# Causal attention on one core: masks as the last products of their step, other tiles behind V

## The chip, the cores and the metric

The kernel runs on one core of a Trainium2 chip. The metric is the device time of one execution in microseconds. The core has five engines with queues of their own: TensorE (PE in the profile; PEld are its weight loads), VectorE (DVE), ScalarE (ACT), GpSimd (POOL) and SyncE (SP), which here only issues DMAs. Each takes its instructions in the order in which they were written and waits on semaphores for the others.

## What is computed

Two half-weight feed-forward layers around an attention layer, on 4 sequences of 1024 tokens with 128 features, all in fp32:

```python
x = x + 0.5 * ffn(layernorm(x), w_gate, w_up, w_down)     # silu(gate) * up, 384 hidden
x = x + attn(layernorm(x), wq, wk, wv, wo)
x = x + 0.5 * ffn(layernorm(x), w_gate, w_up, w_down)

# attn: 16 heads of 64, rotary embedding on q and k
scores = einsum('bhid,bhjd->bhij', q, k) * 64 ** -0.5
scores = where(tril(ones(T, T)), scores, -inf)
probs = softmax(scores)
out = einsum('bhij,bhjd->bhid', probs, v)
return einsum('bto,do->btd', out, wo)
```

## The kernel before

The feed-forward layers (`macaron_half`) are not touched. The change is in `attention`. It works on 32 pairs of heads, 8 for each sequence, in a loop over i with an inner u of 0 and 1 (pair p is 2i + u). Everything is stored transposed: keys in the partitions, queries in the columns.

A pair has 12 **steps** (`STEPS`), numbered from 0. A step takes one block of 128 keys and one half of the queries (512 columns, or fewer where the causal mask cuts them: `first_col`). Steps 0 to 3 belong to the first half, 4 to 11 to the second. In each step TensorE computes, for both heads (h is 0 and 1), the scores of the block into `scores[h]`, one PSUM bank for each head: a **high** product (L541; rounded keys times both parts of the queries) and a **low** product (L547; it also brings in the negated row maximum as a 65th row). In steps 0, 1, 2, 3, 6, 8, 10 and 11 (`DIAG`) the block crosses the diagonal, and a third product (L544), 16-bit, of 128 columns, adds -1e30 above it: the **mask**. Their order in a masked step is high, high, mask, mask, low, low. The low products release ScalarE (`scores_full`), which takes the exponentials of the two heads (L679), and these (`probs_done`) release the banks for the next step's high products. The widths of the score products in steps 0 to 11 are 512, 384, 128, 256, 512, 512, 128, 512, 256, 512, 384 and 512 columns.

Two steps later (`LAG`) the probabilities meet **V** (`times_v`, L567): products of 64 output columns of the array for each head, in fp32, side by side. GpSimd adds the probabilities up (L858 to L862), `sum_probs` (L577) sums them over the keys, `project_out` (L586) is the output projection of a half.

Between these lies work for the pairs ahead:
- **max tiles** (`max_unit`, L530) compute high scores of the next pair once more, with the queries in the partitions, and VectorE takes their row maxima (L752 for a full tile, L756 for one on the diagonal). They are numbered 0 to 25. Units 8 and 25 (`ROWS_UNIT`, L525) transpose the maxima into rows, which VectorE negates (L766) and SyncE sends into the 65th row (`send_max`, L933). The tiles use two banks in turn, so unit k waits until VectorE is through with unit k-2.
- **projections** of q and k for the pair after next (`project`, L504 to L506), rotated by VectorE (L733 to L745), rounded by ScalarE (`round_high`, L659, behind steps 6 and 8) and split by GpSimd (L840); in even pairs (u is 0) four projections of V (L514 to L516), kept by ScalarE (L668).

The tables `MAX_AHEAD`, `MAX_BEHIND`, `MAX_LATE`, `PROJ_AT` and `V_AT` say in which step which unit comes, and `pair` of each engine puts them in order: ahead is between the scores and V, behind is after V.

SyncE's queue for one pair is, in order: `fill_qk(.., 0)` (8 DMAs, L908 and L909, as soon as the scores of the pair before are done), `send_max(p, u, 1)`, which waits for unit 25's negation, `fill_qk(.., 1)` (8), `fill_low` (4, L914 and L915), `copy_v`, `load_wo`, loads, `send_max(p + 1, 1 - u, 0)`. `round_high` writes the tile from which the fills read, so in step 6 it waits for all of them. On ScalarE it is followed by `invert` (L686, L690) and the exponentials of step 7.

Of the kernel before, what the change touches and what calls it, by code (L numbers as in the profile page):

```python
# [21 lines left out]
P = 128  # L22
# [369 lines left out]
def attention(nc, x, xn_dram, xn_stored, wo_pairs, ahead_of, cos, sin, tables_arrived, constants,  # L392
              probs_mem, v_stage, banks):
    ones64, tri_mask, ident, ident16, mask16 = constants
# [3 lines left out]
    with ctx:  # L398
# [54 lines left out]
                     [(1, h, i + b, k) for h in range(2) for i in (4, 6) for k in range(2) for b in range(2)] + [(1, None, None, None)])  # L453
        NT = len(MAX_UNITS)
        ROWS_UNIT = [8, NT - 1]
        MAX_AHEAD = {4: (2, 3), 5: (6, 7), 6: (8, 9), 7: (11,), 8: (13,), 10: (18,), 11: (20, 21)}
        MAX_BEHIND = {3: (0, 1), 4: (4, 5), 6: (10,), 7: (12,), 8: (14, 15), 9: (16, 17), 10: (19,), 11: (22,)}
        MAX_LATE = (23, 24)
        N_QK, N_LOW, N_SENT = 16 * 8, 16 * 4, 16 * 2

        PROJ_AT = {0: 0, 1: 1, 2: 2, 3: 3, 5: 4, 6: 5}
        ROUND_AT, LOW_AT = {6: 0, 8: 1}, {7: 0, 9: 1}
        V_AT = {(0, 7): 0, (0, 8): 1, (0, 9): 2, (0, 11): 3}

        def probs_of(s):
            slot = s % SLOTS
# [2 lines left out]
        def first_col(s):  # L469
            c, j = STEPS[s]  # L470
            return max(0, P * (j - 4 * c))
# [20 lines left out]
        def _(pe):  # L492
# [40 lines left out]
            def score(p, i, u, s):  # L533
                c, j = STEPS[s]
                x0 = first_col(s)
                keys, q = slice(j * P, (j + 1) * P), slice(c * CHUNK + x0, (c + 1) * CHUNK)

                def with_high(h):
                    if some(2 * NS * p + 2 * s + h - 1):
                        pe.wait_ge(probs_done, 2 * NS * p + 2 * s + h - 1)  # L540
                    nc.tensor.matmul(scores[h][:, x0:], k_hh[u][h][:, keys], q_hl[u][h][:, q], start=True, stop=False)  # L541

                def with_mask(h):
                    nc.tensor.matmul(scores[h][:, x0:x0 + P], ident16[:], mask16[:], start=False, stop=False)  # L544

                def with_low(h):
                    nc.tensor.matmul(scores[h][:, x0:], k_l1[u][h][:, keys], q_hm[u][h][:, q], start=False,  # L547
                                     stop=True).then_inc(scores_full, 1)

                if s in DIAG:  # L550
                    for part in (with_high, with_mask, with_low):
                        for h in range(2):
                            part(h)
                else:
                    for h in range(2):
                        with_high(h)
                        with_low(h)

            def times_v(p, u, s):
                c, j = STEPS[s]  # L560
# [20 lines left out]
            def project_out(p, i, u, c):  # L581
                if c == 0:
                    pe.wait_ge(wo_loaded[u], 16 * (i + 1))
                pe.wait_ge(head_done, 2 * p + c + 1)
                pe.wait_ge(norm_free, 4 * p + 2 * c + 1)
                nc.tensor.matmul(norm_bank[:], wo_cur[:, u, :], head_out[:, c, :], start=True, stop=True).then_inc(norm_full, 1)  # L586

            def pair(i, u, first, last):
                p = 2 * i + u
                has_prev, has_next, has_next2 = not (first and u == 0), not (last and u == 1), not last  # L590
                for s in range(NS):
                    if s == 0:
                        if first:
                            pe.wait_ge(ones_done, 4)
                        pe.wait_ge(filled_low[u], N_LOW * (i + 1))
                        pe.wait_ge(v_copied[u], 16 * (i + 1))
                        pe.wait_ge(max_sent[u][0], N_SENT * (i + 1))
                    if s == 4:
                        pe.wait_ge(max_sent[u][1], N_SENT * (i + 1))
                    score(p, i, u, s)  # L600
                    if s == 0 and has_prev:
                        for k in MAX_LATE:
                            max_unit(p, i, u, k)
                    if s == 1 and has_prev:
                        max_unit(p, i, u, ROWS_UNIT[1])
                    if has_next:
                        for k in MAX_AHEAD.get(s, ()):
                            max_unit(p + 1, i + u, 1 - u, k)
                    if s == 4 and has_prev:
                        project_out(p - 1, i - 1 + u, 1 - u, 1)  # L610
                    if s == 8:
                        project_out(p, i, u, 0)
                    if s >= LAG:
                        times_v(p, u, s - LAG)
                    elif has_prev:
                        times_v(p - 1, 1 - u, s - LAG + NS)
                    if s == 2 and has_prev:
                        sum_probs(p - 1, 1)
                    if s == 6:
                        sum_probs(p, 0)  # L620
                    if has_next:
                        for k in MAX_BEHIND.get(s, ()):
                            max_unit(p + 1, i + u, 1 - u, k)
                    if s in PROJ_AT and has_next2:
                        project(i + 1, u, PROJ_AT[s])
                    if (u, s) in V_AT and has_next2:
                        project_v(i + 1, V_AT[u, s])

# [495 lines left out]
```

## Time and profile before

| | |
|---|---|
| median of 3 runs | 1355.13 us (1354.36 to 1357.69) |
| the profiled execution | 1354.49 us, of which the trace's span is 1352.8 us |
| TensorE busy | 1288.6 us, 95% |
| VectorE busy | 871.6 us, 64% |
| GpSimd busy | 752.1 us, 56% |
| ScalarE busy | 618.7 us, 46% |
| mean granted TensorE clock | 0.975 of full |

Times below are microseconds from the start of the span. A row of the instructions in order of time has its start, its length, the engine, the line, and what it writes and reads; rows of the same kind that follow each other are merged (x2), and their length is then from the first start to the last end. The length of a product includes its way through the array, so products overlap in the rows; how far apart they start is what they cost. Attention lies between about 150 and 1240 us. `ident` and `mask` of L544 are the 16-bit tiles.

### The profile page before, as it was taken

The page shows a single profiled execution, that of the slowest core. Times are in us where ns is not written, and L with a number is a line of the kernel's source. Part 1 is how long each engine was busy: PE and PEld are TensorE (multiplying, and loading weights), DVE is VectorE, ACT ScalarE, POOL GpSimd, SP SyncE. Part 2 cuts the span into 40 slices and gives each one's busy share as a digit, 9 for nine tenths or more (in the row PEclk, how much of TensorE's full clock was granted, in tenths as well). Part 3 has the DMA queues.
Part 4 walks back from the last instruction along what each step waited for, and adds up shares of the span by engine and source line. Part 5 has one row for each costly group of instructions (what it writes and reads, how often), then busy time and mean ns, then how long its engine had stood idle before and what let it go on. Part 6 is the DMA issues. An engine that isn't in the chain of part 4 may idle for free. (4 is left out here: it accounts for less than half of the span.)

```text
span 1352.8 us, 24949 instructions
## 1 busy us (share of the span) xinstructions
PE 1288.6 (95%) x6240; PEld 737.4 (55%) x6240; DVE 871.6 (64%) x2270; ACT 618.7 (46%) x1176; POOL 752.1 (56%) x454
## 2 busy tenths in 40 slices
PE   5986689999999999999999999999999999999798
PEld 2543455555555555555555655555555555555365
DVE  5565557767676767676767676767676767664254
ACT  3654134444444444444444444444444444444474
POOL 4123146666666656566666666666666666665300
PEclk8998599999999999999999999999999999999899
DMA  7022556555555646464646464646464646452001
GB/s 280 33 93 72 155 119 159 119 145 132 131 145 120 156 112 163 111 157 118 158 107 163 105 161 107 163 107 162 104 165 105 160 107 162 107 121 56 0 24 39
DMA packets 113612, 165.86 MB, mean 123 GB/s; under 512 B 13360, under 2 KB 63408, under 8 KB 113456
## 3 DMA queue, kind: packets, MB, share of 16 engines
q1 hardware_dynamic: 113584, 165.53, 48.0%
q8 instruction: 12, 0.20, 0.1%
q14 instruction: 16, 0.13, 0.0%
HBM read 37.29 MB, written 10.49 MB: 35 GB/s over the span
## 5 line engine op out<-in xcount | busy, mean ns | idle before, releaser
L862 POOL TENSOR_TENSOR psum_p<-psum_p,shared_a 128x256 f32<-128x256 f32 (+1 forms) x192 | 280.9, 1463 | 93.9 <-ACT shared_a L679 84.4
L679 ACT ACTIVATE shared_a<-bank 128x512 f32<-128x512 f32 (+3 forms) x512 | 201.5, 445 | 240.4 <-PE bank L547 232.8
L530 PE MATMUL bank<-k_hh,q_hl 128*128 128x512 f32 (+3 forms) x768 | 258.7, 392 | 9.7 <-DVE rotated L745 4.2
L547 PE MATMUL bank<-q_hm,k_l 65*128 65x512 f32 (+3 forms) x768 | 243.5, 371 | 0.0
L752 DVE TENSOR_REDUCE max_left<-bank 128x1 f32<-128x512 f32 x256 | 175.7, 687 | 93.3 <-PE bank L530 93.2
L530 PEld LDWEIGHTS bank<-k_hh,q_hl 128*128 128x128 f32 x768 | 138.1, 192 | 173.5 <-issue 72.9
L541 PE MATMUL bank<-q_hl,k_hh 128*128 128x512 f32 (+3 forms) x768 | 227.2, 349 | 0.7 <-ACT shared_a L679 0.5
L679 ACT ACTIVATE probs_more<-bank 128x512 f32<-128x512 f32 (+1 forms) x256 | 132.1, 568 | 191.1 <-PE bank L547 176.8
L756 DVE CUSTOM_DVE_ANT_0 max_scratch<-bank,tri_mask,max_left 128x128 f32<-128x128 f32 (+3 forms) x256 | 137.9, 548 | 109.6 <-PE bank L530 109.6
L567 PE MATMUL bank<-shared_a,v_cur 128*64 128x512 f32 (+3 forms) x1024 | 201.1, 471 | 0.0
L840 POOL TENSOR_TENSOR parts<-rotated,parts 128x1024 fp32r<-128x1024 f32 x64 | 152.4, 2381 | 58.0 <-ACT parts L659 58.0
L860 POOL TENSOR_TENSOR psum_p<-probs_more 128x1024 f32<-128x1024 f32 x32 | 76.1, 2380 | 142.6 <-ACT probs_more L679 142.6
L862 POOL TENSOR_TENSOR psum_p<-psum_p,probs_more 128x768 f32<-128x768 f32 x64 | 134.7, 2105 | 24.4 <-ACT probs_more L679 21.5
L541 PEld LDWEIGHTS bank<-q_hl,k_hh 128*128 128x128 f32 x768 | 131.6, 190 | 24.0 <-ACT shared_a L679 5.9
L756 DVE CUSTOM_DVE_ANT_0 max_scratch<-bank,tri_mask 128x128 f32<-128x128 f32 (+3 forms) x256 | 118.4, 488 | 40.8 <-PE bank L530 39.2
L567 PE MATMUL bank<-probs_more,v_cur 128*64 128x512 f32 (+1 forms) x512 | 131.0, 591 | 0.0
L547 PEld LDWEIGHTS bank<-q_hm,k_l 65*128 65x128 f32 x768 | 126.0, 191 | 7.4
L738 DVE TENSOR_TENSOR bank<-bank,cos 128x256 f32<-128x256 f32 x128 | 54.6, 427 | 77.3 <-PE bank L506 77.2
L567 PEld LDWEIGHTS bank<-shared_a,v_cur 128*64 128x64 f32 x1024 | 50.6, 134 | 92.7 <-ACT probs_more L679 33.1
L659 ACT ACTIVATE parts<-rotated 128x1024 fp32r<-128x1024 f32 x64 | 67.7, 1059 | 68.7 <-DMA q_hm<-parts 56.4
L860 POOL TENSOR_TENSOR psum_p<-shared_a 128x768 f32<-128x768 f32 x32 | 58.4, 1825 | 73.0 <-ACT shared_a L679 73.0
L504 PEld LDWEIGHTS bank<-xn_cur,w_qk 128*128 128x128 f32 x192 | 37.6, 196 | 84.9 <-issue 35.7
(126 smaller groups left out, 1923.0 us busy)
## 6 DMA issues: line engine op xcount, KB each, us to landing
q_hl<-parts SPq DMA_DIRECT2D x256, 128.0 KB, 2.8
k_hh<-parts SPq DMA_DIRECT2D x256, 128.0 KB, 2.7
xn_cur<-xn_scratch SPq DMA_DIRECT2D x16, 1024.0 KB, 6.4
k_l<-parts SPq DMA_DIRECT2D x64, 256.0 KB, 4.9
q_hm<-parts SPq DMA_DIRECT2D x64, 256.0 KB, 5.0
v_cur<-shared_b SPq DMA_DIRECT2D x32, 512.0 KB, 6.0
w_qk<-w_scratch SPq DMA_DIRECT2D x32, 256.0 KB, 3.1
w_scratch<-first_w_parts SPq DMA_DIRECT2D x8, 512.0 KB, 3.1
```

The lines of the kernel that those rows point to most:

```text
L530: nc.tensor.matmul(max_bank[k % 2][:, 0:w], q_hl[u][h][:, q * P:(q + 1) * P], k_hh[u][h][:, keys * CHUNK:keys * CHUNK + w], start=True, st ...
L541: nc.tensor.matmul(scores[h][:, x0:], k_hh[u][h][:, keys], q_hl[u][h][:, q], start=True, stop=False)
L547: nc.tensor.matmul(scores[h][:, x0:], k_l1[u][h][:, keys], q_hm[u][h][:, q], start=False, stop=True).then_inc(scores_full, 1)
L567: last = nc.tensor.matmul(out_bank[c][HEAD_DIM * h:HEAD_DIM * (h + 1), x0:], v_cur[:, u, j, HEAD_DIM * h:HEAD_DIM * (h + 1)], probs_of(s)[ ...
L659: nc.scalar.activation(parts[:, 0, :, c * CHUNK:(c + 1) * CHUNK], rotated[c][:], ACT.Copy).then_inc(high_done, 1)
L679: nc.scalar.activation(probs_of(s)[:, h, x0:], scores[h][:, x0:], ACT.Exp, scale=SCORE_SCALE).then_inc(probs_done, 1)
L738: nc.vector.tensor_tensor(bank[:, w:2 * w], bank[:, 0:w], cos[:, cols], ALU.mult).then_inc(by_cos_done, 1)
L752: nc.vector.reduce_max(max_left[:, col], max_bank[k % 2][:], AX.X).then_inc(max_free, 1)
L756: nc.vector.tensor_tensor_reduce(out=max_scratch[k % 2][:, 0:w], in0=max_bank[k % 2][:, 0:w], in1=tri_mask[:, CHUNK - w:], scale=1.0, scal ...
L840: nc.gpsimd.tensor_tensor(parts[:, 1, :, cols], rotated[c][:], parts[:, 0, :, cols].bitcast(F32), ALU.subtract).then_inc(low_done, 1)
L860: last = nc.gpsimd.tensor_tensor(acc, probs_of(s - 1)[:, :, x0:], new, ALU.add)
L862: last = nc.gpsimd.tensor_tensor(acc, acc, new, ALU.add)
```

## The change

In a masked step the low product of a head now directly follows its high product, as in unmasked steps, and the two masks come last, with the signal to ScalarE. Directly behind them comes V of two steps before. What stood between the scores and V moves: the max tiles of step 0 (23 and 24) and the transposed rows of step 1 (unit 25) go behind V, and so do units 8 and 9 in step 6, and 13 and the output projection in step 8. In steps 10 and 11 one max tile (17, 20) stays ahead, between the low products and the masks. To even this out tiles are dealt out anew in steps 4 to 11. The fourth projection of V moves from step 11 to step 10.

```diff
-        MAX_AHEAD = {4: (2, 3), 5: (6, 7), 6: (8, 9), 7: (11,), 8: (13,), 10: (18,), 11: (20, 21)}
-        MAX_BEHIND = {3: (0, 1), 4: (4, 5), 6: (10,), 7: (12,), 8: (14, 15), 9: (16, 17), 10: (19,), 11: (22,)}
+        MAX_AHEAD = {4: (2, 3), 5: (5,), 7: (11,), 9: (14, 15), 10: (17,), 11: (20,)}
+        MAX_BEHIND = {3: (0, 1), 4: (4,), 5: (6, 7), 6: (8, 9, 10), 7: (12,), 8: (13,), 9: (16,), 10: (18, 19), 11: (21, 22)}
...
-        V_AT = {(0, 7): 0, (0, 8): 1, (0, 9): 2, (0, 11): 3}
+        V_AT = {(0, 7): 0, (0, 8): 1, (0, 9): 2, (0, 10): 3}
...
-                def with_mask(h):
-                    nc.tensor.matmul(scores[h][:, x0:x0 + P], ident16[:], mask16[:], start=False, stop=False)
-
                 def with_low(h):
-                    nc.tensor.matmul(scores[h][:, x0:], k_l1[u][h][:, keys], q_hm[u][h][:, q], start=False,
+                    return nc.tensor.matmul(scores[h][:, x0:], k_l1[u][h][:, keys], q_hm[u][h][:, q], start=False,
+                                            stop=s not in DIAG)
+
+                for h in range(2):
+                    with_high(h)
+                    last = with_low(h)
+                    if s not in DIAG:
+                        last.then_inc(scores_full, 1)
+
+            def mask_scores(s):
+                x0 = first_col(s)
+                for h in range(2):
+                    nc.tensor.matmul(scores[h][:, x0:x0 + P], ident16[:], mask16[:], start=False,
                                      stop=True).then_inc(scores_full, 1)
-
-                if s in DIAG:
-                    for part in (with_high, with_mask, with_low):
-                        for h in range(2):
-                            part(h)
-                else:
-                    for h in range(2):
-                        with_high(h)
-                        with_low(h)
...
                     score(p, i, u, s)
+                    if has_next:
+                        for k in MAX_AHEAD.get(s, ()):
+                            max_unit(p + 1, i + u, 1 - u, k)
+                    if s == 4 and has_prev:
+                        project_out(p - 1, i - 1 + u, 1 - u, 1)
+                    if s in DIAG:
+                        mask_scores(s)
+                    if s >= LAG:
+                        times_v(p, u, s - LAG)
+                    elif has_prev:
+                        times_v(p - 1, 1 - u, s - LAG + NS)
+                    if s == 8:
+                        project_out(p, i, u, 0)
+                    if s == 2 and has_prev:
+                        sum_probs(p - 1, 1)
+                    if s == 6:
+                        sum_probs(p, 0)
                     if s == 0 and has_prev:
                         for k in MAX_LATE:
                             max_unit(p, i, u, k)
                     if s == 1 and has_prev:
                         max_unit(p, i, u, ROWS_UNIT[1])
```

The order on TensorE in step 1 of a pair, before. L541 is high, L544 the mask, L547 low, L525 unit 25, L567 V of the pair before, L504 the projection:

```order
L541 MATMUL bank0<-q_hl10,k_hh10 128x384
L541 MATMUL bank1<-q_hl11,k_hh11 128x384
L544 MATMUL bank0<-mask16,ident16 128x128
L544 MATMUL bank1<-mask16,ident16 128x128
L547 MATMUL bank0<-q_hm10,k_l110 128x384
L547 MATMUL bank1<-q_hm11,k_l111 128x384
L525 MATMUL bank5<-ident,max_all1 128x128
L567 MATMUL bank3<-probs_more,v_cur 64x512 x2
L504 MATMUL bank6<-xn_cur,w_qk 128x256
```

And after the change, on TensorE in the same step (low is now L544, the mask L556):

```order
L541 MATMUL bank0<-q_hl10,k_hh10 128x384
L544 MATMUL bank0<-q_hm10,k_l110 128x384
L541 MATMUL bank1<-q_hl11,k_hh11 128x384
L544 MATMUL bank1<-q_hm11,k_l111 128x384
L556 MATMUL bank0<-mask16,ident16 128x128
L556 MATMUL bank1<-mask16,ident16 128x128
L567 MATMUL bank3<-probs_more,v_cur 64x512 x2
L525 MATMUL bank5<-ident,max_all1 128x128
L504 MATMUL bank6<-xn_cur,w_qk 128x256
```

The masks moved behind the low products, and unit 25 from ahead of V to behind it.

On TensorE from the low products of step 6 to the projection, before. L525 is unit 8, the two L530 are units 9 and 10, L577 the sums:

```order
L547 MATMUL bank0<-q_hm00,k_l100 128x128
L547 MATMUL bank1<-q_hm01,k_l101 128x128
L525 MATMUL bank4<-ident,max_all0 128x128
L530 MATMUL bank5<-k_hh10,q_hl10 128x512
L567 MATMUL bank3<-probs_more,v_cur 64x512 x2
L577 MATMUL bank7<-psum_p,ones64 64x512 x2
L530 MATMUL bank4<-k_hh10,q_hl10 128x512
L504 MATMUL bank6<-xn_cur,w_qk 128x256
```

And on TensorE in the same place after the change:

```order
L556 MATMUL bank0<-mask16,ident16 128x128
L556 MATMUL bank1<-mask16,ident16 128x128
L567 MATMUL bank3<-probs_more,v_cur 64x512 x2
L577 MATMUL bank7<-psum_p,ones64 64x512 x2
L525 MATMUL bank4<-ident,max_all0 128x128
L530 MATMUL bank5<-k_hh10,q_hl10 128x512
L530 MATMUL bank4<-k_hh10,q_hl10 128x512
L504 MATMUL bank6<-xn_cur,w_qk 128x256
```

Units 8 and 9 moved behind V and the sums and now stand directly ahead of unit 10, which uses the bank of unit 8.

## Rows read from the trace of the kernel before

**Rows 1.** Page: busy time (share, instructions); granted clock in 40 slices of 33.8 us.

```profile
PE 1288.6 (95%) x6240; PEld 737.4 (55%) x6240; DVE 871.6 (64%) x2270; ACT 618.7 (46%) x1176; POOL 752.1 (56%) x454
...
PEclk8998599999999999999999999999999999999899
```

**Rows 2.** Waits of PE, 181 to 1238 us: waiter, releaser, total, times, longest.

```profile
PE bank L530 <- DMA k_hh<-parts: 1.6, 1, 1.6
```

**Rows 3.** In order of time, PE: first high products of an even, an odd, an even pair.

```profile
586.52 0.69 PE L541 MATMUL bank<-q_hl,k_hh 128*128 128x512 f32 x2
...
622.34 0.64 PE L541 MATMUL bank<-q_hl,k_hh 128*128 128x512 f32 x2
...
655.33 0.69 PE L541 MATMUL bank<-q_hl,k_hh 128*128 128x512 f32 x2
```

**Rows 4.** In order of time: step 3 of the odd pair, and low's weight loads.

```profile
630.95 0.28 PE L506 MATMUL bank<-xn_cur,w_qk 128*128 128x256 f32 x1
...
631.07 0.40 PE L541 MATMUL bank<-q_hl,k_hh 128*128 128x256 f32 x2
...
631.30 0.28 PE L544 MATMUL bank<-mask,ident 128*128 128x128 bf16 x2
631.37 0.30 PEld L547 LDWEIGHTS bank<-q_hm,k_l 65*128 65x128 f32 x2
...
631.81 0.87 PE L567 MATMUL bank<-shared_a,v_cur 128*64 128x384 f32 x4
```

**Rows 5.** The same, PE, steps 7 and 8: tile, V, tile, high of step 8.

```profile
643.61 0.22 PE L530 MATMUL bank<-k_hh,q_hl 128*128 128x128 f32 x1
643.76 1.08 PE L567 MATMUL bank<-probs_more,v_cur 128*64 128x512 f32 x4
644.77 0.39 PE L530 MATMUL bank<-k_hh,q_hl 128*128 128x256 f32 x1
645.00 0.40 PE L541 MATMUL bank<-q_hl,k_hh 128*128 128x256 f32 x2
```

**Rows 6.** The same, step 1: unit 25, V, its negation, the DMA, the projection.

```profile
626.45 0.27 PE L525 MATMUL bank<-ident,max_all 128*128 128x128 f32 x1
...
626.65 1.08 PE L567 MATMUL bank<-probs_more,v_cur 128*64 128x512 f32 x4
626.97 0.27 DVE L766 TENSOR_SCALAR neg_max_rows<-bank 8x128 fp32r<-8x128 f32 x1
627.27 0.65 SPq L933 DMA_DIRECT2D q_hm<-neg_max_rows  x1
...
627.66 0.39 PE L504 MATMUL bank<-xn_cur,w_qk 128*128 128x256 f32 x1
```

**Rows 7.** The same: the last fill's issue, ScalarE's rounding, exponentials of step 7.

```profile
636.08 0.71 SPq L915 DMA_DIRECT2D q_hm<-parts  x1
...
641.66 1.06 ACT L659 ACTIVATE parts<-rotated 128x1024 fp32r<-128x1024 f32 x1 [1.34 <-DMA q_hm<-parts]
...
643.78 1.06 ACT L679 ACTIVATE shared_a<-bank 128x512 f32<-128x512 f32 x2
```

**Rows 8.** The same, next odd pair: exponentials of step 7, step 8's second high load.

```profile
712.95 1.06 ACT L679 ACTIVATE shared_a<-bank 128x512 f32<-128x512 f32 x2
...
714.07 0.19 PEld L541 LDWEIGHTS bank<-q_hl,k_hh 128*128 128x128 f32 x1 [0.21 <-ACT shared_a L679]
```

**Rows 9.** The same, even pair: exponentials of step 7, high products of step 8.

```profile
608.29 1.07 ACT L679 ACTIVATE shared_a<-bank 128x512 f32<-128x512 f32 x2
...
609.95 0.40 PE L541 MATMUL bank<-q_hl,k_hh 128*128 128x256 f32 x2
```

**Rows 10.** The same, at the start: unit 8, its negation, unit 10's weight load.

```profile
158.54 0.48 PE L525 MATMUL bank<-ident,max_all 128*128 128x128 f32 x1 [0.90 <-DVE max_all L756]
...
159.05 0.28 DVE L766 TENSOR_SCALAR neg_max_rows<-bank 8x128 fp32r<-8x128 f32 x1 [0.57 <-PE bank L525]
...
159.38 0.29 PEld L530 LDWEIGHTS bank<-k_hh,q_hl 128*128 128x128 f32 x1 [0.45 <-DVE neg_max_rows L766]
```

More of the change, by code:

```diff
@@ L605, in pair @@
                         max_unit(p, i, u, ROWS_UNIT[1])
[L606 to L620, printed above, removed]
                     if has_next:
```

## Prediction

> **What bounds the kernel now.** I read the shares of the engines first, then the table of waits, then the instructions in order of time in three pairs of heads. TensorE is busy for 1288.6 of 1352.8 us [rows 1], and while attention runs, from 181 to 1238 us, the longest idle time of TensorE is one of 1.6 us behind a DMA [rows 2]: the reader is to see that it waits for nobody. A pair takes 35.82 us (586.52 to 622.34) when it also projects the next V's, an "even" pair here (u is 0), and 32.99 us (622.34 to 655.33) when it doesn't, an "odd" one [rows 3]. So time goes down only if TensorE's own stream gets shorter, and up whenever another engine's answer comes too late for it. I cost both.
>
> **The masks.** Step 3 shows what they cost. Its first product starts at 631.07, the V product behind it at 631.81 [rows 4]: 0.74 us. A product of 256 columns takes 0.12 (630.95 to 631.07), so four are 0.48 and 0.26 are left for two masks and for the entry into V. The entry alone: a tile of 128 columns (half of 0.12, 0.06) starts at 643.61 and V's at 643.76 [rows 5], 0.15, so 0.09. The masks therefore cost 0.17. The second one starts 0.07 behind the first (the load for the first low product starts with it, at 631.37, the masks begin at 631.30) and the low product can stream only when its 128x128 load is in: 631.81 less the entry and two products is 631.48, 0.11 after 631.37, while a mask streams 0.06. This uncovered load is what the new place removes: behind a low product the mask's own load is covered, and behind the second mask comes V, whose entry is paid anyway. Masks then cost 0.07 + 0.06 = 0.13. I take 0.05 saved (0.04 by this sum, both ends rounded) in a step whose products are 256 columns or wider: steps 0, 1, 3, 8, 10, 11. In steps 2 and 6 the products have 128 columns, and a load of 0.11 behind a product of 0.06 is uncovered each time. In the order high, high, mask, mask, low, low two loads of products are hidden less (0.11 behind the second mask, 0.11 between the lows, 0.11 between the highs); in the order high, low, high, low, mask, mask three are (between the four products), so nothing is saved. Gain: 6 x 0.05 = 0.30 us per pair.
>
> The entry behind a mask is not in this trace. From below: it is swallowed, and V starts with the second mask's end, 0.09 less in all eight masked steps. From above: V's entry starts only when a load like the low product's is through, 0.05 more, and the gain is gone. I take 0.09, since it is 0.09 behind a lone tile of 128 columns [rows 5], the nearest in length to a mask, and also in step 3 by construction. The Trainium skill says of this ("TensorEngine Tiling (Array Packing)", Key Properties) that changing the tiling mode drains the array; V's products use 64 columns of it, everything else 128, which speaks for an entry behind a mask as well. Against the change speaks "TensorE: Matmul & The Clock Gate" (The mechanism): weight loads overlap running products only when their row group differs. By that no load would be covered, masks would cost the same in either place, and the 0.30 would be nothing; but 128x128 loads show 0.19 us [rows 8] where products follow each other every 0.12 us [rows 4], so the trace disagrees and the sum stays.
>
> **Tiles and the output projection that move behind V.** The same products with the same widths; one entry into V and one exit per step as before. The exit costs 0.10 and then about 0.10 of uncovered load, whoever comes first (643.76 to 645.00 in rows 5: V of 512 columns, a tile of 256). If the projection or the transposed rows come first, their first load is another kind; I price that at nothing, with 0.05 either way. VectorE does the same work; adding its durations along its queue I find tile k-2 free before tile k wants its bank in every other step (an estimate; the narrowest is step 11, about 0.2 us). Two places are different.
>
> **Step 6: a new wait.** Units 8, 9 and 10 now stand in one row behind the sums. Unit 10 needs the bank of unit 8, and that is free when VectorE has negated the rows that unit 8 transposed. Before, V and the sums lay between. The start of the kernel has the same three in a row [rows 10]: transposed at 158.54, negated from 159.05 for 0.28, the load for the next tile at 159.38, 0.84 later, and at half the granted clock (the fifth slice, 135 to 169 us, in rows 1), where the small product shows 0.48 us against 0.27 later [rows 6]. So at full clock 0.84 - 0.20 = 0.64, with the load behind V's exit some 0.06 more: 0.70 from transposing to the load of unit 10, and 0.11 more until it streams, since its load waited too: 0.81. Without a wait it would stream after transposing and unit 9: 0.06 + 0.11 + 0.05 + 0.24 = 0.46. The wait is 0.35 us on TensorE's path, in each of the 31 pairs that have a next one. If the load could go ahead of the semaphore it would be 0.24; the load row at 159.38 waited for VectorE itself, so I take 0.35.
>
> **Step 1: the last rows are sent later.** Unit 25 moves behind V of step 1. That product takes 1.01 us (626.65 to 627.66) [rows 6]. Before, VectorE was still rotating when unit 25 ended (626.45 + 0.27 = 626.72) and negated at 626.97, so 0.25 of the delay was idle already. With 0.05 for the mask of step 0 and 0.05 of another first load, the negation comes 1.01 - 0.25 + 0.08 = 0.84 us later (tiles 23 and 24 behind V make the rotation 0.2 later, still before it). SyncE waits for it at 627.27 (send_max) with the second half of the fills queued behind it: eight fill_qk, four fill_low, copy_v, load_wo. The last fill is issued at 636.08 and ScalarE's rounding of step 6 starts at 641.66, released by exactly that DMA after 1.34 us of idling [rows 7]. There is no spare time in this chain, so 0.84 passes on: rounding, invert, exponentials of step 7 (643.78, two of them, to 644.84).
> Who is late then: the second head's product of step 8. Its load could start at 645.00 [rows 5] and its exponential is done and seen at 644.84 + 0.06 = 644.90 (the 0.06: exponentials end at 712.95 + 1.06 = 714.01, the waiting load starts at 714.07 [rows 8], in a pair where the DMA was late enough to show this wait). Spare 0.10; it is now the third product instead of the second, 0.12 more; TensorE itself arrives 0.35 - 3 x 0.05 = 0.20 later. 0.84 - 0.42 = 0.42 us of stall in odd pairs. In even pairs the exponentials end at 608.29 + 1.07 = 609.36 and step 8 starts at 609.95 [rows 9]: 0.53 + 0.12 + 0.20 = 0.85, just enough.
>
> **The sum**, against this execution's own 1354.49 us (span 1352.8 and 1.7 around it; the median of the runs is 1355.13, 0.6 above). Even pairs: -0.30 + 0.35 = +0.05, 16 of them, +0.8. Odd pairs with a DMA chain, 15: -0.15 + 0.35 + 0.42 - 0.15 = +0.47, +7.0. The last pair has neither wait: -0.3. Together +7.5: 1362 us. Its own range is 1357 to 1367: 0.05 either way for the moved first loads on 32 pairs (1.6), the wait of step 6 at 0.24 instead of 0.35 in even pairs (1.8), 0.15 us of scatter in when fills land on 15 pairs (2.3).
>
> **Rivals.** (1) The queue chain has slack that I don't see, for instance fills that land no later because the DMA rings, not SyncE, set their pace. For it: between 636.08 and 641.66 lie 5.6 us, far more than an issue takes. Against: SyncE had nothing in flight but the rows while it waited, so the second half starts later as a whole. Then odd pairs cost as even ones: 1354.5 + 31 x 0.05 - 0.3, about 1355.5, no change. 20%.
> (2) The other side, faster: VectorE's answer in step 6 is covered too, or V starts right behind the mask. With both waits gone only the masks are left, 32 x 0.30 = 9.6, 1345. With the waits there but the entry swallowed, even pairs get 8 x 0.09 = 0.72 shorter (-0.67 in all, 16 of them, -10.7), odd ones keep what comes from step 8 on and before the rows are sent, five entries, 0.45 (+0.02), the last pair gets 1.0: 1343. It decides at a wait below 0.30 in step 6, or an entry below 0.09. 18%.
> (3) The masks' move buys nothing because the load that was uncovered returns ahead of V: even +0.35, odd 0.35 + (0.84 - 0.22 - 0.35) = +0.62: 1354.5 + 5.6 + 9.3 = 1369. It decides at an entry of 0.14 behind a mask. For it: no row shows an entry behind 16-bit products. Another answer that comes too late (the exponentials of a masked step start later by up to a tile) would end here too. 12%.
>
> **How the numbers follow.** Forecast 50%, rivals 20, 18 and 12. 0.3%, 4.1 us, is about what a measurement of this kernel tells from no change: below 1351.1 faster, above 1359.2 slower. The forecast's range lies four fifths above that, so slower 0.40 + 0.12 = 0.52; same 0.10 + 0.20 = 0.30; faster 0.18. The range leaves out the lower half of (2) and most of (3): 1347 to 1367.
>
> **What the profile after would show.** In step 3, 0.69 to 0.70 us from the first high product to V. In step 6 a gap: the load of the second tile of 512 behind the transposed rows waits for the negation, some 0.7 us after them. In step 1 the negation at 5.5 us after the pair's start instead of 4.6, and rounding 0.8 later. In odd pairs the third product of step 8 waits for ScalarE. Even pairs near 35.9 us, odd ones near 33.45. Wrong would be: rounding at its old time (then rival 1), no gap in step 6 or V within 0.1 us of the second mask (rival 2), or waits of scores in other steps than 8.

## The result

The changed kernel takes 1356.97 us (median of 13 runs, 1354.68 to 1360.44) against 1355.13 before; the ratio is 1.0019, with a 95% interval of 1.001 to 1.0028. A second measurement, beside new runs of before, gave 1.0027 (1.0014 to 1.0039). So it is slower, by some 3 us, where 7.5 were forecast: the sign was right, the size more than twice too large, and by the bound of 0.3% that the prediction names it counts as no change.

The page of the profile after, its busy times (share, instructions), against [rows 1]: TensorE is 2.9 us less busy, and the span is 2.5 us longer.

```profile
span 1355.3 us, 24949 instructions
...
PE 1285.7 (95%) x6240; PEld 754.7 (56%) x6240; DVE 870.1 (64%) x2270; ACT 618.8 (46%) x1176; POOL 750.7 (55%) x454
```

The waits of TensorE while attention runs (waiter, releaser, total, times, longest), against [rows 2]. Max tiles that wait for a negation are new. High products waited for an exponential once before, for 0.5 us, and now do so for 2.5 us:

```profile
PE bank L541 <- ACT shared_a L679: 0.5, 1, 0.5
```

And after the change:

```profile
PE bank L530 <- DVE neg_max_rows L768: 3.3, 14, 0.2
PE bank L541 <- ACT shared_a L681: 2.5, 4, 1.7
```

Together these two are 6 us. They understate the waits: the length of a product in the rows includes its way through the array, and idle time is counted only where no product is on its way. What a wait costs is better read from how far apart the steps start. The mean time from the first high product of a step to that of the next, worked out from the starts of all these products (even pairs 2 to 28, odd pairs 1 to 29), in us:

| step | 0 | 1 | 2 | 3 | 4 | 5 | 6 | 7 | 8 | 9 | 10 | 11 | pair |
|---|---|---|---|---|---|---|---|---|---|---|---|---|---|
| before, even | 3.27 | 2.55 | 2.95 | 2.57 | 3.00 | 2.48 | 3.55 | 3.05 | 3.45 | 3.34 | 1.96 | 3.65 | 35.82 |
| after, even | 3.16 | 2.44 | 2.94 | 2.53 | 2.83 | 2.66 | 3.97 | 3.05 | 3.01 | 3.51 | 2.90 | 2.86 | 35.86 |
| before, odd | 3.23 | 2.55 | 2.95 | 2.57 | 3.00 | 2.49 | 3.55 | 2.33 | 2.77 | 2.60 | 2.07 | 2.94 | 33.04 |
| after, odd | 3.14 | 2.44 | 2.94 | 2.53 | 2.83 | 2.66 | 3.88 | 2.50 | 2.62 | 2.78 | 2.13 | 2.91 | 33.36 |

Steps 4 and 5, and 8 to 11, exchange tiles (and a projection of V between 10 and 11), so there only their sums speak: steps 4 and 5 together are unchanged, 0.00 to 0.01.

**The masks**, step 3 of an odd pair in order of time (start, length, engine, line), against [rows 4]: from the first high product, 631.41, to V, 632.11, there are 0.70 us instead of 0.74. The masks start at 631.89 and V 0.22 later: 0.07, 0.06 and an entry of 0.09, as priced.

```profile
631.41 0.28 PE L541 MATMUL bank<-q_hl,k_hh 128*128 128x256 f32 x1
631.53 0.28 PE L544 MATMUL bank<-q_hm,k_l 65*128 65x256 f32 x1
631.65 0.28 PE L541 MATMUL bank<-q_hl,k_hh 128*128 128x256 f32 x1
631.77 0.28 PE L544 MATMUL bank<-q_hm,k_l 65*128 65x256 f32 x1
631.89 0.29 PE L556 MATMUL bank<-mask,ident 128*128 128x128 bf16 x2
632.11 0.54 PE L567 MATMUL bank<-shared_a,v_cur 128*64 128x384 f32 x2
```

**The wait of step 6**, the same pair, against [rows 10]: unit 8 is transposed at 641.92, its negation starts at 642.28, and the weight load of unit 10 sits idle until 642.62, 0.70 after unit 8. That is the 0.70 of the prediction to the hundredth. In the even pair ahead of it the same distance is 0.79 (the rows are at the end of this document).

```profile
641.92 0.33 PE L525 MATMUL bank<-ident,max_all 128*128 128x128 f32 x1
...
642.28 0.28 DVE L768 TENSOR_SCALAR neg_max_rows<-bank 8x128 fp32r<-8x128 f32 x1 [0.63 <-PE bank L525]
...
642.62 0.19 PEld L530 LDWEIGHTS bank<-k_hh,q_hl 128*128 128x128 f32 x1 [0.45 <-DVE neg_max_rows L768]
```

**The late rows**, same pair (it starts at 622.89), against [rows 6, 7]. Unit 25 is transposed at 627.95, negated at 628.31 and sent at 628.62; the negation is 5.42 us behind the pair's start instead of 4.63. The last fill is issued at 637.51, 14.62 behind the start instead of 13.74, and rounding starts at 642.91, 20.02 instead of 19.32. It idles 2.22 us for the fills instead of 1.34, and the exponentials of step 7 follow at 645.03.

```profile
628.31 0.28 DVE L768 TENSOR_SCALAR neg_max_rows<-bank 8x128 fp32r<-8x128 f32 x1 [0.40 <-PE bank L525]
...
628.62 1.32 SPq L935 DMA_DIRECT2D q_hm<-neg_max_rows  x2
...
637.51 0.69 SPq L917 DMA_DIRECT2D q_hm<-parts  x1
...
642.91 1.06 ACT L661 ACTIVATE parts<-rotated 128x1024 fp32r<-128x1024 f32 x1 [2.22 <-DMA q_hm<-parts]
...
645.03 1.06 ACT L681 ACTIVATE shared_a<-bank 128x512 f32<-128x512 f32 x2
```

Who waits for them, in step 8 of this pair: the weight load of the third product starts at 646.14, 0.05 after the second exponential ends (645.03 + 1.06 = 646.09), as in [rows 8], only now in every odd pair. On average 0.36 us of the stall lie at this third product (step 8 takes 2.62 us, and 2.26 in the kernel f1 below, where nothing waits) and 0.17 at the first one, whose exponential is late as well (step 7 takes 2.50 instead of 2.33, from 2.33 to 2.88 in single pairs).

```profile
645.66 0.19 PEld L541 LDWEIGHTS bank<-q_hl,k_hh 128*128 128x128 f32 x1
645.77 0.19 PEld L544 LDWEIGHTS bank<-q_hm,k_l 65*128 65x128 f32 x1
646.14 0.19 PEld L541 LDWEIGHTS bank<-q_hl,k_hh 128*128 128x128 f32 x1 [0.19 <-ACT shared_a L681]
```

### The profile page after: what moved, and what is told of

Read it like the earlier page. It is cut to its first block and busy times, and to the rows that moved or that the text cites. A ratio compares the mean times of both kernels' runs of the same rounds, so it can differ in the third digit from the quotient of the medians.

```text
span 1355.3 us, 24949 instructions
## 1 busy us (share of the span) xinstructions
PE 1285.7 (95%) x6240; PEld 754.7 (56%) x6240; DVE 870.1 (64%) x2270; ACT 618.8 (46%) x1176; POOL 750.7 (55%) x454
## 5 line engine op out<-in xcount | busy, mean ns | idle before, releaser
L530 PE MATMUL bank<-k_hh,q_hl 128*128 128x512 f32 (+3 forms) x768 | 275.7, 407 | 13.8 <-DVE rotated L747 4.4
L541 PE MATMUL bank<-q_hl,k_hh 128*128 128x512 f32 (+3 forms) x768 | 266.7, 354 | 2.8 <-ACT shared_a L681 2.5
L754 DVE TENSOR_REDUCE max_left<-bank 128x1 f32<-128x512 f32 x256 | 172.8, 689 | 149.1 <-PE bank L530 148.1
L544 PE MATMUL bank<-q_hm,k_l 65*128 65x512 f32 (+3 forms) x768 | 262.8, 349 | 0.0
L530 PEld LDWEIGHTS bank<-k_hh,q_hl 128*128 128x128 f32 x768 | 138.1, 194 | 191.4 <-issue 85.2
L567 PE MATMUL bank<-shared_a,v_cur 128*64 128x512 f32 (+3 forms) x1024 | 201.2, 471 | 0.0
L541 PEld LDWEIGHTS bank<-q_hl,k_hh 128*128 128x128 f32 x768 | 146.5, 191 | 31.5 <-ACT shared_a L681 9.3
L544 PEld LDWEIGHTS bank<-q_hm,k_l 65*128 65x128 f32 x768 | 146.4, 191 | 14.3 <-issue 0.2
L567 PE MATMUL bank<-probs_more,v_cur 128*64 128x512 f32 (+1 forms) x512 | 131.0, 591 | 0.0
L567 PEld LDWEIGHTS bank<-shared_a,v_cur 128*64 128x64 f32 x1024 | 50.6, 134 | 58.3 <-ACT probs_more L681 23.8
L504 PE MATMUL bank<-xn_cur,w_qk 128*128 128x256 f32 (+1 forms) x192 | 69.4, 361 | 5.7 <-PEq L114 4.9
```

Source lines behind the costliest of these rows:

```text
L504: nc.tensor.matmul(out, w_qk[:, 0, half], xn_cur[:, 0, xs], start=True, stop=False)
L530: nc.tensor.matmul(max_bank[k % 2][:, 0:w], q_hl[u][h][:, q * P:(q + 1) * P], k_hh[u][h][:, keys * CHUNK:keys * CHUNK + w], start=True, st ...
L544: return nc.tensor.matmul(scores[h][:, x0:], k_l1[u][h][:, keys], q_hm[u][h][:, q], start=False, stop=s not in DIAG)
L567: last = nc.tensor.matmul(out_bank[c][HEAD_DIM * h:HEAD_DIM * (h + 1), x0:], v_cur[:, u, j, HEAD_DIM * h:HEAD_DIM * (h + 1)], probs_of(s)[ ...
L754: nc.vector.reduce_max(max_left[:, col], max_bank[k % 2][:], AX.X).then_inc(max_free, 1)
```

## The experiments

Theory A: the masks' place saves time, and two waits give back more than that: unit 10 for the negation in step 6, and step 8 for exponentials that late rows delay by way of SyncE's queue. Theory B: masks that end a step make the exponentials late, and this is the loss. Ratios are against the kernel before, run beside each on the same chip.

| kernel | ratio (95% interval) | median, us | even pair | odd pair |
|---|---|---|---|---|
| before | 1 | 1353.7 to 1355.1 | 35.82 | 33.04 |
| the change | 1.0019 (1.001 to 1.0028) | 1357.0 | 35.86 | 33.36 |
| e1: masks only | 0.9951 (0.9935 to 0.9967) | 1348.5 | 35.50 | 32.99 |
| e2: change, steps 4 to 6 back | 1.0016 (1.0003 to 1.003) | 1357.4 | 35.66 | 33.40 |
| e3: change, units 23 to 25 ahead | 1.0052 (1.0036 to 1.0068) | 1361.5 | 36.17 | 33.25 |
| e4: change, both back | 0.9985 (0.9973 to 0.9997) | 1352.4 | 35.81 | 32.92 |
| f1: change, SyncE's order | 0.9977 (0.9965 to 0.9989) | 1350.0 | 35.81 | 32.84 |
| f2: the same and steps 4 to 6 back | 0.9899 (0.9881 to 0.9918) | 1339.5 | 35.38 | 32.51 |
| f4: before, units 8 to 10 in a row | 1.0075 (1.0058 to 1.0091) | 1365.5 | 36.25 | 33.37 |
| f5: before, unit 25 behind V | 1.0106 (1.0087 to 1.0125) | 1369.7 | 36.15 | 33.89 |
| g1: before, SyncE's order | 0.9999 (0.9987 to 1.0012) | 1353.4 | 35.80 | 32.99 |

### Masks only (e1)

```diff
                     score(p, i, u, s)
...
+                    if s in DIAG:
+                        mask_scores(s)
                     if s >= LAG:
                         times_v(p, u, s - LAG)
```

`score` and `mask_scores` are those of the change; units 23 to 25, the tiles ahead and the output projection stay ahead of the masks, and the tables are those of before.

> The kernel before with one part of the change alone: high, low, high, low, then the tiles, unit 25 and the output projection ahead of V as before, then the two masks, then V. The tables of tiles are those of before. Theory A (masks next to V save 0.05 us in six steps of each pair, and what the change lost is two waits: unit 10 for VectorE in step 6, and step 8 for exponentials that the late rows of unit 25 delay): neither wait is there, so 32 x 0.3 = 9.6 us less than before, about 1345.5. Theory B (the loss comes from masks that end the step, so that the exponentials start later and the next step's high products wait for their bank): about as slow as the whole change or slower, 1355 to 1358, with high products (L541) waiting for ScalarE in both kinds of pairs.

0.9951, some 6.6 us less, where 9.6 were expected. Theory B is out as the cause of the loss: this kernel has its masks last, too, and is faster. (The traced execution is the slowest of this kernel, 1355.0 us; its first pair starts 3.4 us later than in the trace of before, and the pairs in the middle are compared here.) Even pairs are 0.32 us shorter, as expected, odd ones only 0.05. Two things take the rest.

The larger one is a wait for VectorE in step 10 of odd pairs, which takes 2.20 instead of 2.07 us. Tile 18 stands right behind the score products and needs the bank of tile 16. With the masks gone from ahead of it, its turn comes 0.18 us after the start of the last score product, at 653.94, but its load starts at 654.13, 0.89 us behind the step's first product. In the kernel before it is 0.89 as well, in every odd pair, and there, too, VectorE is what the load waits for:

```profile
651.21 0.19 PEld L530 LDWEIGHTS bank<-k_hh,q_hl 128*128 128x128 f32 x1 [0.17 <-DVE max_all L756]
```

And with the masks alone moved:

```profile
653.76 0.33 PE L544 MATMUL bank<-q_hm,k_l 65*128 65x384 f32 x1
...
654.13 0.19 PEld L530 LDWEIGHTS bank<-k_hh,q_hl 128*128 128x128 f32 x1 [0.34 <-DVE max_all L758]
```

So nothing can be saved ahead of tile 18, and the masks, now behind it, add their 0.13. From V to the next step both kernels take 0.75. In even pairs tile 18 starts 0.71 behind, without a wait, and step 10 is 0.06 shorter (1.90). The wait costs the kernel before something as well: its load is late, and V follows tile 18 after 0.43 us in odd pairs, 0.33 in even ones. The change asks for tile 17 there and 18 behind V, and shows no such wait (step 10: 2.13 with one more tile of 512 columns behind V).

The smaller one is step 11, in both kinds of pairs no shorter than before (3.66 against 3.65 and 2.95 against 2.94), where 0.05 was priced. Here Theory B fits: the exponentials of step 10 start at 654.88 and are over at 655.75, and the load for the second head's high product starts at 655.80, about the distance that a waiting load showed in [rows 8], though its row names no releaser.

### The change, steps 4 to 6 back (e2)

```diff
-        MAX_AHEAD = {4: (2, 3), 5: (5,), 7: (11,), 9: (14, 15), 10: (17,), 11: (20,)}
+        MAX_AHEAD = {4: (2, 3), 5: (6, 7), 6: (8, 9), 7: (11,), 9: (14, 15), 10: (17,), 11: (20,)}
-        MAX_BEHIND = {3: (0, 1), 4: (4,), 5: (6, 7), 6: (8, 9, 10), 7: (12,), 8: (13,), 9: (16,), 10: (18, 19), 11: (21, 22)}
+        MAX_BEHIND = {3: (0, 1), 4: (4, 5), 6: (10,), 7: (12,), 8: (13,), 9: (16,), 10: (18, 19), 11: (21, 22)}
```

> The change, but in steps 4 to 6 the tiles stand as before (6, 7 ahead of V in step 5; 8 and 9 ahead in step 6, 10 behind), so that unit 10 no longer follows unit 8 directly. Theory A: even pairs lose their wait of 0.35 us (16 x 0.35 = 5.6); odd pairs are set by the queue chain up to step 8, so they gain nothing (their stall in step 8 grows by what step 6 gives back). 5 to 6 us less than the whole change, about 1351. Theory B: no more than 1 us less.

Step 6 is down to 3.54 in both kinds of pairs: the wait is gone, 0.43 in even and 0.34 in odd pairs. But the kernel is no faster than the change (1.0016 against 1.0019), where 5 to 6 us less were expected. In odd pairs step 7 takes 2.89 instead of 2.50: all of it comes back as waiting for ScalarE, as A expected. In even pairs 0.20 come back in step 8, which A had not: their spare time, 0.85 us against 0.84 of delay in the prediction, rested on the very 0.35 of waiting that this edit takes away. The gain per even pair, 0.20, shows in the traces, where the last pair starts 1067.14 us after the first instead of 1069.23; the two intervals are too wide to tell these 2 us.

### The change, units 23 to 25 ahead (e3)

```diff
                     score(p, i, u, s)
+                    if s == 0 and has_prev:
+                        for k in MAX_LATE:
+                            max_unit(p, i, u, k)
+                    if s == 1 and has_prev:
+                        max_unit(p, i, u, ROWS_UNIT[1])
...
-                    if s == 0 and has_prev:
-                        for k in MAX_LATE:
-                            max_unit(p, i, u, k)
-                    if s == 1 and has_prev:
-                        max_unit(p, i, u, ROWS_UNIT[1])
```

> The change, but units 23, 24 and 25 stand ahead of the masks and V as before, so that SyncE sends the rows 0.8 us earlier. Theory A: the fills land 0.7 to 0.8 us earlier, the stall of 0.46 us in step 8 of the 15 odd pairs is gone (6.9 us), the wait in step 6 stays: about 1350, even and odd pairs both near their times of before. Theory B: slower than the change, since masks of steps 0 and 1 now end later.

The expected time, about 1350, was wrong (1361.5), though the expected mechanism is there: steps 7 and 8 of odd pairs fall from 5.12 to 4.62 us, so the stall is gone. But the kernel got slower, for step 0 takes 3.47 instead of 3.16 in all pairs. In order of time, step 0 of an odd pair:

```profile
625.82 0.19 PEld L530 LDWEIGHTS bank<-k_hh,q_hl 128*128 128x128 f32 x1
...
626.41 0.19 PEld L530 LDWEIGHTS bank<-k_hh,q_hl 128*128 128x128 f32 x1 [0.41 <-DVE max_left L754]
```

Unit 24's load waits for VectorE, which is not through with unit 22. The change had moved units 21 and 22 behind V of step 11, and with 23 and 24 ahead of V of step 0 four tiles are asked for within one step. So the new place of units 23 and 24 wasn't free to choose: the dealt-out tables need it.

### The change, both back (e4)

> The change with both of these put back: tiles of steps 4 to 6 and units 23 to 25 as before. Theory A: only what the masks save is left, 9.6 us less than before, about 1345.5, pairs 0.3 us shorter than before in both kinds. If the two parts each bring 5.6 and 6.9 and don't add up, a third wait takes over. Theory B: as e2.

Both edits above in one. 0.9985: the wait of step 0 (3.48) stands where the two others were. Without it, 0.31 in each pair, this would be 35.50 and 32.61. So A's first answer, 1345.5, is missed by 7 us, and its second holds: a third wait takes over.

### The change, SyncE's order (f1)

```diff
                     fill_qk(1 - u, 0)
+                    fill_qk(1 - u, 1, (0,))
                 if not (first and u == 0):
                     send_max(p, u, 1)
                 if has_next:
-                    fill_qk(1 - u, 1)
+                    fill_qk(1 - u, 1, (1,))
```

The new last argument of `fill_qk` names the heads, four DMAs for each.

> The change with another order in SyncE's queue alone: four of the eight DMAs of fill_qk(1 - u, 1) now stand ahead of send_max(p, u, 1), so that the late rows no longer hold up the fills. TensorE's order is that of the change. Theory A (queue chain: late rows, late fills, late rounding, late exponentials of step 7, stall in step 8 of odd pairs): rounding in step 6 starts some 2 us earlier, odd pairs lose all of their 0.46 us in steps 7 and 8 (32.9 instead of 33.36), even pairs stay at 35.86 with the wait in step 6: about 7 us less than the change, 1349 to 1350. Rival: the stall comes from ScalarE's own load or from masks that end step 7's neighbours: no change.

This leaves TensorE's order alone and takes the late rows out of the way of half of the fills behind them. 0.9977, against 1.0019 and 1.0027 for the change: 6 to 7 us less, as expected. In the odd pair that starts at 619.53 the last fill is issued at 632.22, 12.69 behind the start instead of 14.62, and rounding waits 0.32 for it instead of 2.22; the exponentials of step 7 now wait for TensorE's low product, not for the invert ahead of them:

```profile
632.22 0.64 SPq L917 DMA_DIRECT2D q_hm<-parts  x1
...
637.65 1.06 ACT L661 ACTIVATE parts<-rotated 128x1024 fp32r<-128x1024 f32 x1 [0.32 <-DMA q_hm<-parts]
...
640.77 1.08 ACT L681 ACTIVATE shared_a<-bank 128x512 f32<-128x512 f32 x2 [0.76 <-PE bank L544]
```

Odd pairs get 0.52 us shorter, all in steps 7 and 8 (4.59 instead of 5.12), and step 6 keeps its wait (3.87). That shows the queue chain as the cause of the stall.

### The change, SyncE's order and steps 4 to 6 back (f2)

> As f1_sync_order, and in steps 4 to 6 the tiles as before (the edit of e2_steps4to6_back), so that both waits are gone. Theory A: even pairs 35.4, odd ones 32.5, 0.4 and 0.5 less than before; 12 to 14 us less than before, about 1342. If the edit of e2 again brings nothing, the reading of e2 (that the queue chain took its gain) is wrong.

Both waits gone: 1339.5 us, 14.3 less than before, the fastest kernel here (12 to 14 less were expected). The edit that brought nothing in the change brings 10 us here, since its gain no longer ends at the queue chain. Of the waits of TensorE in attention one of note is left, in the first pair:

```profile
PE bank L541 <- ACT shared_a L681: 1.2, 1, 1.2
PE bank L530 <- DVE max_all L758: 0.4, 2, 0.3
```

### Before, units 8 to 10 in a row (f4)

```diff
-        MAX_AHEAD = {4: (2, 3), 5: (6, 7), 6: (8, 9), 7: (11,), 8: (13,), 10: (18,), 11: (20, 21)}
+        MAX_AHEAD = {4: (2, 3), 5: (6, 7), 7: (11,), 8: (13,), 10: (18,), 11: (20, 21)}
-        MAX_BEHIND = {3: (0, 1), 4: (4, 5), 6: (10,), 7: (12,), 8: (14, 15), 9: (16, 17), 10: (19,), 11: (22,)}
+        MAX_BEHIND = {3: (0, 1), 4: (4, 5), 6: (8, 9, 10), 7: (12,), 8: (14, 15), 9: (16, 17), 10: (19,), 11: (22,)}
```

> The kernel before with one part of the change alone: units 8, 9 and 10 in a row behind the sums of step 6. Theory A: unit 10's load waits for the negation of unit 8, 0.35 us in step 6 of each of 31 pairs, less some 0.03 to 0.05 for a cheaper first load behind the sums: +9 to +11 us, 1363 to 1366. Rival (the answer of VectorE is covered): no change.

1.0075, +11.6 us against expected +9 to +11. Only step 6 grows, by 0.43 in even and 0.33 in odd pairs. The wait is a part of the change by itself.

### Before, unit 25 behind V (f5)

```diff
-                    if s == 1 and has_prev:
-                        max_unit(p, i, u, ROWS_UNIT[1])
...
                     elif has_prev:
                         times_v(p - 1, 1 - u, s - LAG + NS)
+                    if s == 1 and has_prev:
+                        max_unit(p, i, u, ROWS_UNIT[1])
```

> The kernel before with one part of the change alone: unit 25 behind V of step 1. Theory A: negation, rows, fills and rounding come 0.95 us later; the stall in step 8 is 0.95 less the spare time: 0.85 us in odd pairs (spare 0.10), 0.4 in even pairs (spare 0.53), less 0.05 in each pair for the cheaper first load behind V: +16 to +18 us, about 1371. Rival (the chain has slack): no change.

1.0106, +15.8 us, just below the expected +16 to +18. One transposing of 128 columns, moved from ahead of V to behind it, costs more than the whole change. Odd pairs are 0.85 longer, even ones 0.33, in steps 7 and 8. In order of time, weight loads of step 8 in an odd pair: both high products wait for their exponentials.

```profile
654.18 0.19 PEld L541 LDWEIGHTS bank<-q_hl,k_hh 128*128 128x128 f32 x1 [0.24 <-ACT shared_a L679]
654.67 0.19 PEld L541 LDWEIGHTS bank<-q_hl,k_hh 128*128 128x128 f32 x1 [0.30 <-ACT shared_a L679]
```

Step 1 itself is 0.05 shorter (2.50 instead of 2.55), which the prediction had put at nothing. By how far apart the products start, unit 25 takes 0.12 us ahead of V (0.38 from the last low product to V, 0.26 without it) and 0.07 behind V (from V to the projection's second product 1.30 instead of 1.23). Whether its cheaper load or the way into V makes the difference was not tested.

### Before, SyncE's order (g1)

> Control: the kernel before with SyncE's new order alone (four fills ahead of send_max). Theory A: in the kernel before the queue chain has just enough time (0.10 us spare in a median odd pair; a few odd pairs lose 0.25), so that faster fills bring nothing but these few: 0 to 1 us less. Rival (SyncE's order is worth something by itself, and the gain of f1 and f2 has nothing to do with the change): 5 us or more less.

0.9999. Without late rows the fills have time enough, so the gain of the two kernels above comes from the chain that the change made critical. Odd pairs are 0.05 shorter: in the kernel before five of them have a step 8 of 2.75 to 3.01 us instead of 2.72, here the mean is 2.72.

### The change again (g2)

> The change itself once more, beside runs of before on the same chip, for a second trace and a second interval: 1 to 4 us more than before; even pairs 35.86, odd pairs 33.36, from the first to the last pair's start some 4 us more. If the first trace was an outlier, the odd pairs' stall in steps 7 and 8 (0.5 us) or the even pairs' wait in step 6 is smaller here.

1.0027; even pairs 35.85, odd ones 33.31, and from the first pair's start to the last one's 1068.19 us, against 1069.23 in the first trace and 1064.98 (and 1063.73 with SyncE's order) for before. The steps agree with the first trace to 0.04.

## Why the prediction was wrong

**Right: the masks.** 0.04 to 0.06 in a wide step where no other engine is waited for (0.10 in step 0 of even pairs), an entry of 0.09 behind a mask, 0.01 in steps 2 and 6. (For these two steps the prediction says that two loads are hidden less in the old order and lists three; three against three is what gives its nothing. It also gives V alone 64 columns of the array; the sums have 128*64 in the rows as well.) Masks alone give 0.32 in even pairs (0.30 forecast), but only 0.05 in odd ones, where tile 18 waits for VectorE. The Trainium skill's rule that a change of the tiling mode drains the array ("TensorEngine Tiling (Array Packing)", Key Properties) agrees with the trace behind 16-bit products as well: V starts 0.22 after the first mask, 0.09 more than the two masks take. Whether these 0.09 are the drain or V's own first load was not tested. The Trainium skill's rule that weight loads overlap products only in other row groups ("TensorE: Matmul & The Clock Gate", The mechanism) would have made the masks' move worth nothing; the kernel with masks only is 0.5% faster, so the measurement decides against it here.

**Right: the wait of step 6.** 0.35 forecast; 0.33 in odd pairs, 0.42 in even ones, in the change and alone. The row gave the 0.70 from unit 8 to unit 10's load exactly in odd pairs; in even ones it is 0.79. With this wait there and V 0.22 behind the first mask, rival 2 is out.

**Right: the queue chain.** Late by 0.84 at the negation (0.80 on average over the odd pairs), 0.84 at the rounding (0.79), a stall of 0.42 at the third product of step 8 of odd pairs (0.36 there, and 0.17 at the first product, which the prediction took to be in time), none in even ones (0.04). Of these 0.53 the kernel before has 0.05 already, in its few late pairs (g1), so against it the stall counts 0.48. Rival 1, slack in the chain, is refuted by f5 and f1; rival 3, that the masks' move buys nothing, by e1.

**Wrong: "a tile that moves costs the same", priced at nothing with 0.05 either way.** This is the term of the sum that was mis-sized. The order of the products alone gained more than the masks' 0.30: with both waits taken away an odd pair takes 32.51, 0.48 less than in the kernel before with the same order of SyncE (32.99), an even one 35.38, 0.42 less (35.80). So beyond the masks the new order saves 0.1 in even and 0.2 in odd pairs. Steps 0 to 5 together are 0.25 shorter instead of 0.15: 0.05 of it is unit 25 in step 1 (f5), the rest lies in step 0, which is 0.09 to 0.11 shorter where 0.05 was priced; what does that was not isolated. In odd pairs steps 8 to 11 together are 0.24 shorter when nothing stalls (10.09 in f1 against 10.33 in g1), where 0.15 was priced. The other 0.1 is the wait of tile 18 for VectorE in step 10 of the kernel before, which the change takes away. The prediction had found "tile k-2 free before tile k wants its bank in every other step" by adding durations, and this step is where that was wrong.

An odd pair thus came out as -0.25 (steps 0 to 5) + 0.33 (step 6) + 0.48 (the stall) - 0.24 (steps 8 to 11) = +0.32 instead of -0.15 + 0.35 + 0.42 - 0.15 = +0.47. Over 15 pairs this is 2.3 of the 3.7 us between the forecast and the sum by what was measured, below.

**Wrong: the ends.** The first pair and the last two were counted by rule and not looked at. Pair 30 projects nothing. Its step 6 took 3.71 us before, longer than the 3.55 of pairs that also project in it, so it seems to have waited already, and it takes 3.52 after; step 1 is 0.19 shorter, steps 8 to 11 together 0.28. In all it went from 30.58 to 30.03, and to 30.07 in the second trace, where +0.05 was forecast. The last pair gained 0.47 instead of 0.3. The first pair was 0.5 shorter, but it runs in part at the lower level of the granted clock (0.50 from 172 to 175 us in the trace of before) and took 36.5 to 39.8 us over the kernels here, so its 0.5 says nothing. These ends are 1.3 of the 3.7 us.

The sum by what was measured: 14 x 0.04 + 15 x 0.32 - 0.5 - 0.55 - 0.47 = +3.8 us, against +7.5. The traced executions differ by less still, 2.5 us: the first pair starts at 170.60 instead of 171.98, ahead of everything that was changed, and over the twelve traces this start lies between 170.1 and 175.4. That part is chance. With forecast terms that were each within about 0.1 us per pair, the result still came out at half: gains and losses of 0.3 to 0.5 nearly cancel, and an error of 0.1 in their difference is 3 us over 31 pairs. The range of 1347 to 1367 held the time, and 1356.97 lies just at the lower edge of the forecast's own range, 1357 to 1367. That range allowed 0.05 in each pair for moved first loads, where 0.1 to 0.2 were gained, and nothing for the ends.

## What to carry to other kernels

When one engine is busy all the time, a reordering is priced by two lists: what its own stream saves (here 0.4 to 0.5 us per pair, worth 14 us) and which answers of others it now asks for sooner or delivers later. The smallest instruction can head the longest chain: follow what is queued behind whoever waits for it, through the DMA queue and back. And a wait removed alone may show nothing while a second one, a few us further on, stands ready to take its place; test such edits together as well as apart. Look in the kernel before, too, for loads that wait: one that TensorE's table of waits doesn't show cost 0.1 us in each odd pair.

## What the runs showed of the hardware

A weight load that waits costs time though TensorE shows none idle. In step 10 of the kernel before the load of tile 18 is at work before the last score product ends in even pairs, and V starts 0.33 us after the tile. In odd pairs the load waits for VectorE (0.17 us idle) until that product has streamed, and V starts 0.43 after the tile. An even pair, and an odd one:

```profile
617.45 0.19 PEld L530 LDWEIGHTS bank<-k_hh,q_hl 128*128 128x128 f32 x1
...
617.62 0.40 PE L530 MATMUL bank<-k_hh,q_hl 128*128 128x512 f32 x1
617.95 0.65 PE L567 MATMUL bank<-shared_a,v_cur 128*64 128x256 f32 x4
...
651.21 0.50 PE L530 MATMUL bank<-k_hh,q_hl 128*128 128x512 f32 x1
651.64 0.65 PE L567 MATMUL bank<-shared_a,v_cur 128*64 128x256 f32 x4
```

Where a small product stands changes its cost: unit 25, an fp32 product of 128 columns with a load of 0.14 us, takes 0.12 us ahead of V and 0.07 behind it (f5).

The same instructions in the same order answer at different speed in the two kinds of pairs: unit 8's negation starts 0.36 us after the transposing in the odd pair above (641.92 to 642.28) and 0.46 after it in the even pair before it, though VectorE idles ahead of it in both. Unit 25 shows the same after the change, 0.37 and 0.46 on average.

```profile
606.12 0.33 PE L525 MATMUL bank<-ident,max_all 128*128 128x128 f32 x1
...
606.58 0.28 DVE L768 TENSOR_SCALAR neg_max_rows<-bank 8x128 fp32r<-8x128 f32 x1 [0.72 <-PE bank L525]
...
606.91 0.50 PE L530 MATMUL bank<-k_hh,q_hl 128*128 128x512 f32 x1 [0.24 <-DVE neg_max_rows L768]
```

Step 6 grew by 0.42 there instead of 0.33, in all four kernels with this wait alike (the change, e3, f1, f4). The cause was not tested and stays open.
